# Pair matrices of the switched attention multiplied with two tiles at a time

## Chip, cores and metric

The kernel runs on one core of a Trainium2 chip. The metric is the device time of one execution in microseconds (us); lower is better.

## What is computed

The reference is a stack of eight blocks on x of shape (128, 64, 128), each added to x through a gate. Only the last one matters here, a switched attention with 8 heads, 8 experts a head and two of them chosen a row, once for the values and once for the output:

```python
gate_v = _get_sel_gate(x, sel_v_w, rs)          # sigmoid, top 2 of 8, normed
gate_o = _get_sel_gate(x, sel_o_w, rs)
q = jnp.einsum('bsd,hpd->bhsp', x, q_w.reshape(H, P, D))
k = jnp.einsum('bsd,hpd->bhsp', x, k_w.reshape(H, P, D))
xv = jnp.einsum('bsd,hedp->bshep', x, v_w.reshape(H, E, D, P))
v = jnp.einsum('bshep,bshe->bhsp', xv, gate_v)
att = jax.nn.softmax(jnp.einsum('bhqp,bhkp->bhqk', q, k) * SCALE, axis=-1)
ctx = jnp.einsum('bhqk,bhkp->bqhp', att, v)
weighted = ctx[:, :, :, None, :] * gate_o[..., None]
out = jnp.einsum('bshep,hepd->bsd', weighted, o_w.reshape(H, E, P, D))
```

Here x is layer-normed before it goes in.

## The kernel before

The earlier blocks fill the first 1210 us or so of the execution and are not touched. The last block is `switch_attention`. It works on 64 tiles of 128 rows (two sequences of 64). It is written as a software pipeline by hand: each engine has a list of steps with a lag, and `straight` walks slots t = 0, 1, 2, ... and in each slot runs every step of the list, in the order of the list, for tile t - lag. All waits are semaphores between engines; each engine runs its list in order.

What happens to a tile, with the lag before the change:

- lag 0 and 1: DVE and POOL work out the layer norm; `turn_x` (TensorE, into `sw_m`) turns the tile, and `keep_x` (ACT) copies it out of `sw_m` twice, as `sw_xT` and, rounded, as `sw_xT_high`. `low_x` (POOL) makes `sw_xT_low`, the difference of the two.
- lag 1: `logits` and `exp_logits` give the routing logits, and 20 small DVE operations, `route` (R[0] to R[19], lines 2126 to 2147), the gates. `pair_keys` (TensorE) multiplies the turned tile with the eight pair matrices `sw_pair` (query matrix times key matrix of a head, kept in f32), four heads into each of the two banks `sw_w`; `keep_u` (ACT) copies each bank to `sw_uT`; `scores` multiplies that with the turned tile.
- lag 2: the v units. A unit (`unit`, line 2221) is one head: six matmuls of 128x512, three into a bank `sw_a` and three into a bank `sw_d` (high times high, high times low, low times high), with two banks of each kind in turn. ACT scales the four experts of `sw_a` (`scale`, line 1962), DVE the four of `sw_d` and adds them up (`mix`, line 2117), and POOL adds the rest (`add_v`, lines 1889 and 1894) to give `sw_v`. `context` (line 2267) multiplies the values with the turned probabilities, into the same two banks `sw_w`, and needs `sw_v` of all eight heads.
- lag 3: the o units, the same with the context, and `add_o` on POOL. `finish` on POOL at lag 4.

A unit may start only when the unit two before it has been scaled and mixed (its banks), and ACT may scale a unit only when POOL has added the unit four before it (the four buffers `sw_scaled`). TensorE's list in a slot is

```python
stages = vs[:2] + [(1, turn_x), turns[0], vs[2], turns[1], (1, logits), vs[3], vs[4], (1, pair_keys(0))]
stages += [vs[5], (1, pair_keys(1)), vs[6], vs[7], os[0], (1, scores), os[1], (2, context)]
stages += os[2:]
```

and POOL's is add_v(0), add_v(1), low_x, finish, add_v(2) to add_v(7), add_o(1) and on.

## Time and profile before

| | |
|---|---|
| Time, median of 3 runs | 3166.97 us (3166.52 to 3173.21) |
| The profiled execution | 3168.74 us, of it a span of 3167.0 us |
| Busy: PE, PEld | 2907.0 us (92%), 2176.0 us (69%) |
| Busy: DVE, ACT, POOL | 2780.7 us (88%), 2341.8 us (74%), 2322.8 us (73%) |
| Mean granted TensorE clock | 0.941 |

PE is TensorE's matmuls, PEld its weight loads, DVE is VectorE, ACT ScalarE and POOL GpSimd. Busy is the time in which at least one instruction of the engine ran. A matmul's end is modelled and neighbours overlap, so waits shorter than some tenths of a microsecond don't show as idle on PE; they are read from the distance between starts.

### The profile page before, as it was taken

Reading aid. Unit: us, or ns where it says so; the run is one execution under the profiler, and the core shown is the slowest. Engines: PE = TensorE matmul, PEld = TensorE weight load, DVE = VectorE, ACT = ScalarE, POOL = GpSimd, SP = SyncE. Lnnn points to the kernel's source line nnn. Section 1 sums busy time; section 2 is a strip of 40 time slices with the busy share of each in tenths; the row PEclk is TensorE's granted clock in tenths of the full one; section 3 lists DMA queues with packets and bytes.
Section 4 is the critical chain, followed back from the end, with each engine's and each line's share of the span. In section 5 each row is a group of like instructions: output and inputs, shape, how many; then the busy total and the mean of one; then the engine's idle time right before and its main releaser. Section 6 shows DMA issues by size and latency. Waiting matters only on the chain.

```text
span 3167.0 us, 78218 instructions
## 1 busy us (share of the span) xinstructions
PE 2907.0 (92%) x24620; PEld 2176.0 (69%) x24620; DVE 2780.7 (88%) x9085; ACT 2341.8 (74%) x7546; POOL 2322.8 (73%) x3112
## 2 busy tenths in 40 slices
PE   7489992897689996999999999999999999999998
PEld 7257762675357774677777777777777777777776
DVE  6789997899989986888888888898898898898897
ACT  4866668888976665777777777777777777777776
POOL 2799994666876662677777777777777777777777
PEclk8589995898789997999999999999999999999999
DMA  4000000220000004100000000000000000000000
GB/s 131 8 2 2 2 2 18 68 75 13 1 6 16 16 16 109 30 9 8 7 9 8 7 9 8 7 9 8 7 9 8 8 9 8 7 9 8 7 8 6
DMA packets 114508, 55.31 MB, mean 17 GB/s; under 512 B 18352, under 2 KB 113712, under 8 KB 114096
## 3 DMA queue, kind: packets, MB, share of 16 engines
q1 hardware_dynamic: 114096, 50.30, 5.8%
q8 instruction: 200, 3.28, 0.4%
q14 instruction: 212, 1.74, 0.2%
HBM read 41.81 MB, written 8.45 MB: 16 GB/s over the span
## 4 chain that ended last, share of the span: by engine, by line
PE 59%; DVE 1%; ACT 1%; POOL 1%; DMA 0%; issue 0%; SPq 0%; POOLq 0%; ACTq 0%; DVEq 0%
PE ps_sw_a L2221 24%; PE ps_sw_d L2221 22%; PE ps_sw_w L2267 4%; PE ps_sw_w L2254 3%; PE ps_sw_s L2236 2%; PE ps_sw_s L2278 2%; PE ps_sw_m L2243 1%; ACT sw_scaled L1962 0%; DVE sw_v_part L2117 0%; PE ps_sw_m L2229 0%; DMA sw_v<-in_L_ffn_v_w 0%; POOL sw_v_pair L1889 0%; DVE sw_v_low L2056 0%; DVE sw_o_low L2063 0%; ACT sw_v_high L2017 0%
## 5 line engine op out<-in xcount | busy, mean ns | idle before, releaser
L1962 ACT ACTIVATE sw_scaled<-ps_sw_a,sw_gate_o 128x128 f32<-128x128 f32 x2048 | 620.3, 447 | 254.1 <-PE ps_sw_a L2221 247.0
L1962 ACT ACTIVATE sw_scaled<-ps_sw_a,sw_gate_v 128x128 f32<-128x128 f32 x2048 | 597.3, 448 | 196.2 <-PE ps_sw_a L2221 194.4
L2117 DVE SCALAR_TENSOR_TENSOR sw_o_part<-ps_sw_d,sw_gate_o,sw_o_part 128x128 f32<-128x128 f32 x1920 | 555.6, 339 | 63.1 <-PE ps_sw_d L2221 60.5
L1889 POOL TENSOR_TENSOR sw_v_pair<-sw_v_part,sw_scaled 128x256 f32<-128x256 f32 x512 | 381.9, 746 | 157.0 <-DVE sw_v_part L2117 91.6
L2117 DVE SCALAR_TENSOR_TENSOR sw_v_part<-ps_sw_d,sw_gate_v,sw_scaled 128x128 f32<-128x128 f32 x1024 | 303.9, 337 | 126.1 <-PE ps_sw_d L2221 107.1
L1915 POOL TENSOR_TENSOR sw_o_rest<-sw_o_rest,sw_scaled 128x256 f32<-128x256 f32 x384 | 285.4, 743 | 158.0 <-ACT sw_scaled L1962 120.7
L2117 DVE SCALAR_TENSOR_TENSOR sw_v_part<-ps_sw_d,sw_gate_v,sw_v_part 128x128 f32<-128x128 f32 x1024 | 304.8, 339 | 0.0
L1918 POOL TENSOR_TENSOR sw_o_rest<-sw_o_rest,sw_scaled 128x256 f32<-128x256 f32 x384 | 282.6, 736 | 30.1
L1894 POOL TENSOR_TENSOR sw_v<-sw_v_pair 128x128 f32<-128x128 f32 x512 | 244.6, 478 | 40.1
L1014 POOL TENSOR_TENSOR at_key_wide<-at_keyT,c_half_heads 128x1024 f32<-128x1024 f32 x128 | 242.6, 1895 | 4.6 <-ACT at_keyT L1112 4.6
L2221 PE MATMUL ps_sw_a<-sw_v_high,sw_xT_high 128*128 128x512 f32 x512 | 234.5, 458 | 8.2 <-DVE sw_v_low L2056 8.2
L2221 PE MATMUL ps_sw_a<-sw_o_high,sw_ctx_high 128*128 128x512 f32 x512 | 215.7, 421 | 0.2 <-ACT sw_scaled L1962 0.2
L2221 PE MATMUL ps_sw_d<-sw_v_high,sw_xT_high 128*128 128x512 f32 x512 | 207.6, 405 | 0.3 <-DVE sw_v_part L2117 0.3
L2221 PE MATMUL ps_sw_d<-sw_o_high,sw_ctx_high 128*128 128x512 f32 x512 | 202.1, 395 | 1.2 <-DVE sw_v_part L2117 1.2
L2221 PE MATMUL ps_sw_d<-sw_o_low,sw_ctx_high 128*128 128x512 f32 x512 | 202.7, 396 | 0.0
L2221 PE MATMUL ps_sw_a<-sw_o_high,sw_ctx_low 128*128 128x512 f32 x512 | 202.7, 396 | 0.0
L2221 PE MATMUL ps_sw_a<-sw_v_high,sw_xT_low 128*128 128x512 f32 x512 | 202.5, 396 | 0.0
L2221 PE MATMUL ps_sw_a<-sw_v_low,sw_xT_high 128*128 128x512 f32 x512 | 202.2, 395 | 0.0
L2221 PE MATMUL ps_sw_d<-sw_o_high,sw_ctx_low 128*128 128x512 f32 x512 | 202.1, 395 | 0.0
L2221 PE MATMUL ps_sw_a<-sw_o_low,sw_ctx_high 128*128 128x512 f32 x512 | 202.1, 395 | 0.0
L2221 PE MATMUL ps_sw_d<-sw_v_high,sw_xT_low 128*128 128x512 f32 x512 | 201.8, 394 | 0.0
L2221 PE MATMUL ps_sw_d<-sw_v_low,sw_xT_high 128*128 128x512 f32 x512 | 200.7, 392 | 0.0
...
## 6 DMA issues: line engine op xcount, KB each, us to landing
re_values<-in_ctx SPq DMA_DIRECT2D x128, 64.0 KB, 2.4
...
```

What stands on the lines that cost most here:

```text
L1014: pool.tensor_tensor(key_wide[:, s], keyT[:, s].unsqueeze(1).broadcast_to([P, HALF, P]), C["half_heads"][:].unsqueeze(2).broadcast_to([P, ...
L1889: pool.tensor_tensor(v_pair[:, h % 2], v_part[:, h], scaled[:, h % 4, 2:4], ALU.add)\
L1894: pool.tensor_tensor(v[:, h], v_pair[:, h % 2, 0], v_pair[:, h % 2, 1], ALU.add).then_inc(q["v"], 1)
L1915: pool.tensor_tensor(o_rest[:, 0:2], o_rest[:, 0:2], scaled[:, h % 4, 0:2], ALU.add)\
L1918: pool.tensor_tensor(o_rest[:, 2:4], o_rest[:, 2:4], scaled[:, h % 4, 2:4], ALU.add)\
L1962: act.activation(scaled[:, h % 4, e], ps_a[h % 2][:, e], ACT.Copy, scale=gates[:, s, h, HALF_E + e:HALF_E + e + 1]).then_inc(a_scaled[kind ...
L2117: dve.scalar_tensor_tensor(out=acc[:, e % 2], in0=ps_d[h % 2][:, e], scalar=gates[:, s, h, e:e + 1], in1=before, op0=ALU.mult, op1=ALU.add ...
L2221: m = pe.matmul(bank, lhs[a], w[b][:, h, experts], start=c == 0, stop=c == 2)
L2236: m = pe.matmul(ps_s[t, h], probs[t, s, h], C["ident"][t, t], start=True, stop=True)
L2254: m = pe.matmul(ps_w[n][:, h * P:(h + 1) * P], W["pair"][:, 4 * n + h], xT[:, s], start=True, stop=True)
L2267: m = pe.matmul(ps_w[b][:, h * S:(h + 1) * S], v[t, h], probs_T[t, h], start=True, stop=True)
L2278: m = pe.matmul(ps_s[t], xT[:, s, t], uT[:, :, t], start=True, stop=True)
```

## The change

`pair_keys` takes two turned tiles at once: each pair matrix is loaded once for 256 columns, where it was loaded once a tile for 128. It runs only for even tiles, in two groups of four matmuls of 128x256: heads 0 to 3 at the end of the even slot in which the second tile was turned (lag 2), heads 4 to 7 in the middle of the odd slot after (lag 3). `keep_u` becomes four copies for each pair of tiles, two at the start of the odd slot and two in its middle. Since two tiles must be turned before, everything behind `turn_x` comes two slots later: v units at lag 4, o units at lag 5, `finish` at lag 6. `sw_xT` has four buffers. The rounded copy is taken out of `keep_x` and becomes `round_x`, at lag 3, from `sw_xT` and behind v unit 4 in ACT's list. The routing buffers are shared and `sw_place` is read with a broadcast, to make room in SBUF.

```diff
-        xT = k.sb("sw_xT", [P, 2, P])
+        xT = k.sb("sw_xT", [P, 4, P])
...
-        uT = k.sb("sw_uT", [P, SH, P])
+        uT = k.sb("sw_uT", [P, SH, 2, P])
...
+        def of_pair(step):
+            def at(i, s, rd):
+                if i % 2 == 0:
+                    step(i, s, rd)
+            return at
...
-                straight([(0, fetch), (1, only_first(fetch_v)), (1, only_first(fetch_o(0, 4))), (2, fetch_residual),
-                          (2, only_first(fetch_o(4, 10))), (3, only_first(fetch_o(10, 16))), (4, store)])
+                straight([(0, fetch), (1, only_first(fetch_v)), (1, only_first(fetch_o(0, 4))), (4, fetch_residual),
+                          (2, only_first(fetch_o(4, 10))), (3, only_first(fetch_o(10, 16))), (6, store)])
...
-                stages = [(2, add_v(0)), (2, add_v(1)), (1, low_x), (4, finish)] + [(2, add_v(h)) for h in range(2, SH)]
-                stages += [(3, add_o(h)) for h in range(6)] + [(0, rstd)] + [(3, add_o(h)) for h in range(6, SH)]
+                stages = [(4, add_v(0)), (4, add_v(1)), (3, low_x), (6, finish)] + [(4, add_v(h)) for h in range(2, SH)]
+                stages += [(5, add_o(h)) for h in range(6)] + [(0, rstd)] + [(5, add_o(h)) for h in range(6, SH)]
...
                 def keep_x(i, s, rd):
                     act.wait_ge(q["x_turned"], i + 1)
+                    if not first(i, 4):
+                        act.wait_ge(q["scores"], i - 3)
+                        act.wait_ge(q["xT_low"], i - 3)
+                    act.activation(xT[:, i % 4], ps_m[:, 0], ACT.Copy).then_inc(q["xT"], 1)
+
+                def round_x(i, s, rd):
+                    act.wait_ge(q["xT"], i + 1)
                     if not first(i, 2):
-                        act.wait_ge(q["scores"], i - 1)
                         act.wait_ge(q["xT_low"], i - 1)
                         act.wait_ge(d_made["v"], SH * (i - 1))
-                    act.activation(xT[:, s], ps_m[:, 0], ACT.Copy).then_inc(q["xT"], 1)
-                    act.activation(xT_high[:, s], ps_m[:, 0], ACT.Copy).then_inc(q["xT_high"], 1)
+                    act.activation(xT_high[:, s], xT[:, i % 4], ACT.Copy).then_inc(q["xT_high"], 1)
...
                 def keep_u(n):
                     def step(i, s, rd):
                         act.wait_ge(q["u"], 2 * i + n + 1)
-                        if n == 0 and not first(i, 1):
+                        if n == 0 and i:
                             act.wait_ge(q["scores"], i)
-                        act.activation(uT[:, 4 * n:4 * n + 4], ps_w[n].rearrange("p (h t) -> p h t", h=4), ACT.Copy)\
-                            .then_inc(q["uT"], 1)
-                    return step
+                        act.activation(uT[:, 2 * n:2 * n + 2], ps_w[n % 2].rearrange("p (h c t) -> p h c t", h=2, c=2),
+                                       ACT.Copy).then_inc(q["uT"], 1)
+                    return of_pair(step)
...
-                exps = [(1, lambda i, s, rd, lo=lo: exp_scores(i, s, rd, lo)) for lo in range(0, SH, 2)]
-                vs, os = ([(lag, scale(kind, h)) for h in range(SH)] for kind, lag in (("v", 2), ("o", 3)))
-                stages = vs[:2] + [(1, keep_x)] + vs[2:4] + [(1, exp_logits), (2, keep_probs)] + vs[4:6]
-                stages += [(1, keep_u(0)), vs[6], (1, keep_u(1)), vs[7]] + os[:3] + [(2, keep_ctx(0)), os[3], exps[0]]
-                stages += [os[4], (2, keep_ctx(1)), os[5], exps[1], os[6], exps[2], os[7], exps[3]]
+                exps = [(3, lambda i, s, rd, lo=lo: exp_scores(i, s, rd, lo)) for lo in range(0, SH, 2)]
+                vs, os = ([(lag, scale(kind, h)) for h in range(SH)] for kind, lag in (("v", 4), ("o", 5)))
+                stages = [(3, keep_u(0)), vs[0], (3, keep_u(1)), vs[1], (1, keep_x)] + vs[2:4] + [(3, exp_logits), (4, keep_probs)]
+                stages += [vs[4], (3, round_x), vs[5], (3, keep_u(2)), vs[6], (3, keep_u(3)), vs[7]] + os[:3]
+                stages += [(4, keep_ctx(0)), os[3], exps[0], os[4], (4, keep_ctx(1)), os[5], exps[1], os[6], exps[2], os[7], exps[3]]
...
-                            lambda: dve.tensor_tensor(r["eq1"][:], r["p"][:], wide(rm["m1"][:]), ALU.is_equal),
-                            lambda: dve.tensor_tensor(r["w1"][:], r["eq1"][:], place[:], ALU.mult),
...
+                            lambda: dve.tensor_tensor(r["equal"][:], p[:], wide(rm["m1"][:]), ALU.is_equal),
+                            lambda: dve.tensor_tensor(r["equal"][:], r["equal"][:], place[:].unsqueeze(1).broadcast_to(G), ALU.mult),
...
-                R = [[(1, route(n))] for n in range(RANK)]
+                         for kind, lag in (("v", 4), ("o", 5)) for h in range(SH)}
+
+                R = [[(3, route(n))] for n in range(RANK)]
...
                 def turn_x(i, s, rd):
                     pe.wait_ge(q["xhat"], i + 1)
-                    if not first(i, 1):
-                        pe.wait_ge(q["decays"], i)
+                    if i >= 1:
+                        pe.wait_ge(q["xT"], i)
+                    if i >= 3:
+                        pe.wait_ge(q["decays"], i - 2)
                     pe.transpose(ps_m[:, 0], L["xhat"][:, s], C["ident"][:]).then_inc(q["x_turned"], 1)
...
-                    pe.wait_ge(q["xT_high"], i + 1)
-                    pe.matmul(ps_m[:, 1], xT[:, s], W["sel"][:], start=True, stop=True).then_inc(q["logits"], 1)
-
-                def pair_keys(n):
+                    pe.wait_ge(q["xT"], min(i + 3, TILES))
+                    pe.matmul(ps_m[:, 1], xT[:, i % 4], W["sel"][:], start=True, stop=True).then_inc(q["logits"], 1)
+
+                def pair_keys(lo):
                     def step(i, s, rd):
-                        if i == 0:
-                            pe.wait_ge(prep["kept"], 2 + n)
-                        elif not first(i, 2):
-                            pe.wait_ge(q["ctx_low"], 2 * (i - 2) + n + 1)
-                        else:
-                            pe.wait_ge(q["uT"], 1 + n)
-                        for h in range(4):
-                            m = pe.matmul(ps_w[n][:, h * P:(h + 1) * P], W["pair"][:, 4 * n + h], xT[:, s],
-                                          start=True, stop=True)
-                        m.then_inc(q["u"], 1)
-                    return step
+                        if lo == 0:
+                            pe.wait_ge(q["xT"], i + 2)
+                        for n in (lo, lo + 1):
+                            if n >= 2:
+                                pe.wait_ge(q["uT"], 2 * i + n - 1)
+                            elif i == 0:
+                                pe.wait_ge(prep["kept"], 3)
+                            else:
+                                pe.wait_ge(q["ctx_low"], 2 * (i - 2) + n + 1)
+                            both = xT[:, i % 4:i % 4 + 2].rearrange("p c t -> p (c t)")
+                            for h in range(2):
+                                m = pe.matmul(ps_w[n % 2][:, 2 * h * P:2 * (h + 1) * P], W["pair"][:, 2 * n + h], both,
+                                              start=True, stop=True)
+                            m.then_inc(q["u"], 1)
+                    return of_pair(step)
...
                 def context(i, s, rd):
-                    upto = min(i + 2, TILES) if isinstance(i, int) else i + 2
-                    wait_alone(pe, (q["v"], SH * i + SH), (q["p_kept"], i + 1), (q["uT"], 2 * upto))
-                    if isinstance(i, int) and i == TILES - 1:
+                    wait_alone(pe, (q["v"], SH * i + SH), (q["p_kept"], i + 1))
+                    if i % 2 and i < TILES - 1:
+                        pe.wait_ge(q["uT"], 2 * (i + 3))
+                    elif i:
                         pe.wait_ge(q["ctx_low"], 2 * i)
+                    else:
+                        pe.wait_ge(q["uT"], 4)
...
-                    waits = [(q["uT"], 2 * i + 2)]
+                    waits = [(q["uT"], 4 * (i // 2) + 4)]
...
-                        m = pe.matmul(ps_s[t], xT[:, s, t], uT[:, :, t], start=True, stop=True)
+                        m = pe.matmul(ps_s[t], xT[:, i % 4, t], uT[:, :, s, t], start=True, stop=True)
...
-                vs, os = ([(lag, unit(kind, h)) for h in range(SH)] for kind, lag in (("v", 2), ("o", 3)))
-                turns = [(2, lambda i, s, rd, lo=lo: turn_probs(i, s, rd, lo)) for lo in (0, 4)]
-                stages = vs[:2] + [(1, turn_x), turns[0], vs[2], turns[1], (1, logits), vs[3], vs[4], (1, pair_keys(0))]
-                stages += [vs[5], (1, pair_keys(1)), vs[6], vs[7], os[0], (1, scores), os[1], (2, context)]
-                stages += os[2:]
+                vs, os = ([(lag, unit(kind, h)) for h in range(SH)] for kind, lag in (("v", 4), ("o", 5)))
+                turns = [(4, lambda i, s, rd, lo=lo: turn_probs(i, s, rd, lo)) for lo in (0, 4)]
+                stages = vs[:2] + [(1, turn_x), turns[0], vs[2], turns[1], (3, logits), vs[3], vs[4], (3, pair_keys(2))]
+                stages += vs[5:] + [os[0], (3, scores), os[1], (4, context)] + os[2:] + [(2, pair_keys(0))]
```

TensorE in a middle slot, before, from v unit 4 to v unit 6 (sw_w is the bank of `pair_keys`); the same rows stand in every slot:

```order
L2221 MATMUL ps_sw_d<-sw_v_high,sw_xT_low 128x512
L2254 MATMUL ps_sw_w<-sw_xT,sw_pair 128x128 x4
L2221 MATMUL ps_sw_a<-sw_v_high,sw_xT_high 128x512
L2221 MATMUL ps_sw_a<-sw_v_low,sw_xT_high 128x512
L2221 MATMUL ps_sw_a<-sw_v_high,sw_xT_low 128x512
L2221 MATMUL ps_sw_d<-sw_v_high,sw_xT_high 128x512
L2221 MATMUL ps_sw_d<-sw_v_low,sw_xT_high 128x512
L2221 MATMUL ps_sw_d<-sw_v_high,sw_xT_low 128x512
L2254 MATMUL ps_sw_w<-sw_xT,sw_pair 128x128 x4
```

TensorE of the changed kernel, an odd slot, from the end of v unit 4; an even slot has no row of `sw_pair` here, and has this row behind its last o unit instead:

```order
L2233 MATMUL ps_sw_d<-sw_v_low,sw_xT_high 128x512
L2233 MATMUL ps_sw_d<-sw_v_high,sw_xT_low 128x512
L2272 MATMUL ps_sw_w<-sw_xT,sw_pair 128x256 x4
L2233 MATMUL ps_sw_a<-sw_v_high,sw_xT_high 128x512
L2233 MATMUL ps_sw_a<-sw_v_low,sw_xT_high 128x512
```

So the even slot's middle loses both groups, the odd slot's middle keeps one of twice the columns, and the end of the even slot gains one.

ACT in the first half of a slot, before:

```order
L1962 ACTIVATE sw_scaled<-ps_sw_a,sw_gate_v 128x128 x8
L1972 ACTIVATE sw_xT<-ps_sw_m 128x128
L1973 ACTIVATE sw_xT_high<-ps_sw_m 128x128
L1962 ACTIVATE sw_scaled<-ps_sw_a,sw_gate_v 128x128 x8
L1985 ACTIVATE sw_exp<-ps_sw_m 128x128
L1979 ACTIVATE sw_probs_T<-ps_sw_s 128x512
L1962 ACTIVATE sw_scaled<-ps_sw_a,sw_gate_v 128x128 x8
```

and in the same place of an even slot of the changed kernel:

```order
L1968 ACTIVATE sw_scaled<-ps_sw_a,sw_gate_v 128x128 x8
L1977 ACTIVATE sw_xT<-ps_sw_m 128x128
L1968 ACTIVATE sw_scaled<-ps_sw_a,sw_gate_v 128x128 x8
L1996 ACTIVATE sw_exp<-ps_sw_m 128x128
L1990 ACTIVATE sw_probs_T<-ps_sw_s 128x512
L1968 ACTIVATE sw_scaled<-ps_sw_a,sw_gate_v 128x128 x4
L1984 ACTIVATE sw_xT_high<-sw_xT 128x128
L1968 ACTIVATE sw_scaled<-ps_sw_a,sw_gate_v 128x128 x12
```

`sw_xT_high` has moved from behind two v units (eight activations) to behind five. POOL's list has not moved: `low_x`, which reads `sw_xT_high`, still stands behind add_v(1), with `finish` and add_v(2) to add_v(7) behind it.

## Rows read from the trace of the kernel before

**Rows 1.** Windows: length, busy us of PE, PEld, DVE, ACT, POOL; clock, DMA share, GB/s.
```profile
1313.44:3091.00 1777.56, 1777.23 (x10982) 1361.00 (x10980) 1595.50 (x5701) 1353.20 (x5283) 1359.30 (x2101) 1.00 0.03 8
```

**Rows 2.** Tile sw_xhat: turn_x, one a slot, durations ns, first and last start.
```profile
L2229 PE MATMUL ps_sw_m<-c_ident,sw_xhat x64: 270/271/477, 1225.1 to 3091.0; 128*128 128x128 f32 x64
```

**Rows 3.** Timeline, PE, one slot: start us, us, engine line op out<-in.
```profile
2030.58 1.05 PE L2254 MATMUL ps_sw_w<-sw_xT,sw_pair 128*128 128x128 f32 x8
2031.39 0.48 PE L2221 MATMUL ps_sw_a<-sw_v_high,sw_xT_high 128*128 128x512 f32 x1
2031.70 0.40 PE L2221 MATMUL ps_sw_a<-sw_v_low,sw_xT_high 128*128 128x512 f32 x1
2031.93 0.39 PE L2221 MATMUL ps_sw_a<-sw_v_high,sw_xT_low 128*128 128x512 f32 x1
...
2040.25 0.39 PE L2221 MATMUL ps_sw_d<-sw_o_high,sw_ctx_low 128*128 128x512 f32 x1
2040.73 2.00 PE L2267 MATMUL ps_sw_w<-sw_probs_T,sw_v 64*128 64x64 f32 x32
```

**Rows 4.** Line 1894: who waited for sw_v (us, times).
```profile
  PEld ps_sw_w L2267: 32.1, 64
```

**Rows 5.** Timeline, DVE, same slot, v units 3 to 7.
```profile
2029.82 0.61 DVE L2117 SCALAR_TENSOR_TENSOR sw_v_part<-ps_sw_d,sw_gate_v,sw_scaled 128x128 f32<-128x128 f32 x2 [1.52 <-ACT sw_scaled L1962]
...
2033.29 0.59 DVE L2117 SCALAR_TENSOR_TENSOR sw_v_part<-ps_sw_d,sw_gate_v,sw_scaled 128x128 f32<-128x128 f32 x2
...
2034.93 0.81 DVE L2132 TENSOR_TENSOR sw_r_sel<-sw_r_w,sw_m_w 128x128 f32<-128x128 f32 x1
...
2036.18 0.28 DVE L2133 SCALAR_TENSOR_TENSOR sw_r_p<-sw_r_sel,sw_r_p 128x128 f32<-128x128 f32 x1
...
2038.65 0.60 DVE L2117 SCALAR_TENSOR_TENSOR sw_v_part<-ps_sw_d,sw_gate_v,sw_v_part 128x128 f32<-128x128 f32 x2
```

**Rows 6.** Timeline, POOL, same slot.
```profile
2028.06 0.46 POOL L1881 TENSOR_TENSOR sw_xT_low<-sw_xT,sw_xT_high 128x128 fp32r<-128x128 f32 x1
...
2030.53 0.72 POOL L1889 TENSOR_TENSOR sw_v_pair<-sw_v_part,sw_scaled 128x256 f32<-128x256 f32 x1
...
2031.75 0.74 POOL L1889 TENSOR_TENSOR sw_v_pair<-sw_v_part,sw_scaled 128x256 f32<-128x256 f32 x1
...
2039.40 0.74 POOL L1889 TENSOR_TENSOR sw_v_pair<-sw_v_part,sw_scaled 128x256 f32<-128x256 f32 x1 [1.00 <-DVE sw_v_part L2117]
2040.22 0.46 POOL L1894 TENSOR_TENSOR sw_v<-sw_v_pair 128x128 f32<-128x128 f32 x1
```

**Rows 7.** Timeline, ACT, same slot.
```profile
2030.37 1.18 ACT L1962 ACTIVATE sw_scaled<-ps_sw_a,sw_gate_v 128x128 f32<-128x128 f32 x4
2032.37 1.14 ACT L1962 ACTIVATE sw_scaled<-ps_sw_a,sw_gate_v 128x128 f32<-128x128 f32 x4 [0.82 <-PE ps_sw_a L2221]
2033.38 0.62 ACT L1993 ACTIVATE sw_uT<-ps_sw_w 128x512 f32<-128x512 f32 x1
```

**Rows 8.** Timeline, PE, start of the slot: the two halves of v unit 0.
```profile
2021.49 0.47 PE L2221 MATMUL ps_sw_a<-sw_v_high,sw_xT_high 128*128 128x512 f32 x1
...
2022.26 0.49 PE L2221 MATMUL ps_sw_d<-sw_v_high,sw_xT_high 128*128 128x512 f32 x1
```

**Rows 9.** Timeline, ACT and PE, the beginning of the block.
```profile
1225.77 0.27 ACT L1973 ACTIVATE sw_xT_high<-ps_sw_m 128x128 fp32r<-128x128 f32 x1
...
1236.00 2.04 ACT L2017 ACTIVATE sw_v_high<-sw_v_part 128x1024 fp32r<-128x1024 f32 x2
...
1250.09 0.48 PE L2229 MATMUL ps_sw_m<-c_ident,sw_xhat 128*128 128x128 f32 x1 [6.76 <-DVE sw_xhat L259]
...
1313.44 0.27 PE L2229 MATMUL ps_sw_m<-c_ident,sw_xhat 128*128 128x128 f32 x1
```

**Rows 10.** Timeline, DVE, two of the 16 pieces of o weights.
```profile
1251.71 0.68 DVE L2063 TENSOR_TENSOR sw_o_low<-sw_o_part,sw_o_high 128x512 fp32r<-128x512 f32 x1
1253.49 0.69 DVE L2063 TENSOR_TENSOR sw_o_low<-sw_o_pair,sw_o_high 128x512 fp32r<-128x512 f32 x1
```

42 lines of the change are left out of this document (21 added, 21 removed).

## The prediction

> **What bounds the kernel now.** The rows by engine over the middle of the last block come first: from 1313.44 to 3091.0 us TensorE is busy 1777.23 of 1777.56 us at a granted clock of 1.00, VectorE 90% and POOL and ACT 76% each [rows 1]. So TensorE looks like the only bound. `turn_x` runs once a slot; from 1313.44 to 3091.0 there are 60 slots, 29.63 us each [rows 2, 9]. But the profile's matmuls overlap, and shares don't say what TensorE's order is tied to. For that I read one slot on every engine, the one from 2021.5 to 2051, and all times of day below are of it.
>
> The reader is to see a second chain that takes as long as TensorE's. `context` needs `sw_v` of all heads. POOL's last add of the v units ends at 2040.22 + 0.46 = 2040.68, and `context` starts at 2040.73 [rows 3, 6]; after a first-bank matmul the usual distance is some 0.33 us, so 2040.58 would have been TensorE's own time. Over the whole run its weight load waited for that add 64 times, 0.5 us each [rows 4]: the two meet in every slot with about a tenth of a us between them. Behind POOL stands VectorE: its v units 3 to 7 with the routing between them run without an idle row from 2029.82 to 2038.65 + 0.60 = 2039.25 [rows 5], and POOL's last add waited 1.00 us for it [rows 6]. From 2029.82 to `context` neither has room.
>
> **What the change does to each part.**
>
> *The pair matrices themselves.* A group of four 128x128 matmuls takes 2031.39 - 2030.58 = 0.81 us, and the next matmul's successor comes after 0.31 instead of 0.23 us [rows 3], so 0.89 us a group and 3.56 us for the four groups of two tiles. A group of four of 256 columns does the same columns as two of these: at most 1.78 us, and if the extra 0.08 us of the restart is paid once, 1.70. I take 1.74, so 3.48 us for two tiles: 0.08 us saved in a pair of slots. Halving the weight loads saves nothing further, since PEld is 77% busy beside a full PE [rows 1].
>
> *Even slot, middle.* Here 1.78 us of matmuls go away between v unit 4 and v unit 6. TensorE would be ready for `context` at 2038.8. VectorE's chain is not shortened: it had no idle, so v unit 7 is mixed at 2039.25 and `sw_v` complete at 2040.68 as before. The two groups were covered by VectorE's work, and taking them away gives nothing here.
>
> *Even slot, end.* The new group stands behind the last o unit, where TensorE has nobody's work to hide behind: 1.74 us on the path. It covers something: the halves of v unit 0 start 2022.26 - 2021.49 = 0.77 us apart [rows 8], where three matmuls of 0.23 take 0.69 [rows 3]. That 0.08 us is a wait for the last o units to be scaled and mixed; all four halves of v units 0 and 1 have one, some 0.3 us together, which the group absorbs. Net 1.45 us a pair of slots.
>
> *The rounded copy.* This is the step that I expect to cost most by itself. `low_x` on POOL started at 2028.06 [rows 6]. It will wait for `round_x`, which ACT reaches behind v unit 4: that starts at 2030.37, its successor's copy follows a unit's start by 2033.38 - 2032.37 = 1.01 us [rows 7], so `round_x` runs from 2031.38 and, at the 0.27 us of the same copy with nothing beside it [rows 9], ends at 2031.65. Queued behind `low_x` on POOL are `finish` and add_v(2) to add_v(7). From the start of `low_x` to that of add_v(2) are 2.47 us, from one add_v to the next 1.22, and the last takes 1.28 to the end of `sw_v` [rows 6]. So: 2031.70 + 2.47 + 5 x 1.22 + 1.28 = 2041.55, `context` at 2041.60. TensorE's own time is 2040.58: 1.0 us late, in every slot. POOL's slack of 2.6 us (its waits for ACT and VectorE between the adds) is what the other part of the delay of 3.6 us goes into. For the port (next paragraph) I add 0.1: 1.1 us in even slots.
>
> *Port.* VectorE's L2132 took 0.81 us, against 0.28 for L2133 of the same shape and also with two inputs in SBUF [rows 5]; it lay beside a POOL add, of 0.74 us [rows 6]. Two of the routing operations in this stretch are so long in each slot. With POOL busy without a pause from 2031.7 to 2041.6 some more of the routing will meet an add; I take 0.4 us more on VectorE, which the even slot hides.
> The Trainium skill (SBUF — State Buffer, Terms) says that VectorE and GpSimd share a port pair that is locked for the whole instruction, "the loser fully blocks"; by that rule, read strictly, each of VectorE's two-input operations in this stretch could lose up to an add's 0.74 us. The trace agrees for L2132 and not for most others, so it is a rival below and not the sum.
>
> *Odd slot, middle.* One group of 1.74 us stands before v unit 5, where 0.89 stood before and 0.89 after it. V unit 5 comes 0.85 us later on TensorE, so its mix, before at 2033.29 [rows 5], starts at about 2034.1 and VectorE, without slack, ends v unit 7 at 2040.05; with 0.4 us for the port, 2040.45. POOL gets to that add at 2031.70 + 2.47 + 5 x 1.22 = 2040.27, so it waits 0.2 more, and any more on VectorE goes through: 1.1 + 0.3 = 1.4 us in odd slots.
>
> *No cost.* The four `keep_u` of an odd slot are as many copies as the two of each slot before; the two at its start fall into the time that ACT gains by the group. `sw_place` by broadcast and routing in place keep the number and shape of operations. `logits` waits for the next but one tile's `keep_x`, which stands where it stood.
>
> *Beginning and end.* Two more slots without matmul units. Rounding of the v weights began at 1236.00, behind the exponentials of tile 0, though tile 0 was turned and copied at 1226 [rows 9]; these now come two slots later, so the weights are ready up to 9 us sooner. Against this, the 16 pieces of o weights, before beside units, now stand before the first unit: VectorE's first two are 1.78 us apart [rows 10], of which the units between took half; at 1.4 us each 22 us, and 4 us of routing and exponentials. `turn_x` of the first slot with units: 1250 - 9 + 22 + 4 = 1267. That slot has no o units: 22 us, and the next 30.9. The steady state begins at 1320 instead of 1313.4: 7 us, between -5 and +20. The end is the same chain of units as before.
>
> **The sum.** A pair of slots costs 1.1 + 1.4 + 1.45 = 3.95 us; 0.08 us saved is already in the 1.74. There are 31 such pairs: 122 us. With 7 for the beginning, 129 us on a span of 3167.0 gives 3296. The profiled execution took 3168.74 us and the median is 3166.97, so I give the median as 3296 us. Its own range is 3262 to 3325: the end term lies between 1.2 and 1.78, the two context terms between 0.9 and 1.8.
>
> **The rivals.**
>
> *Only one of the two terms appears.* If ACT or POOL have room that I don't see (a faster restart of the adds, `round_x` earlier because ACT is ahead in even slots), only the group at the slot's end counts: 31 x 1.45 + 7 = 52, 3219 us. If VectorE and POOL are so late at the end of the slot that they take the group in, only POOL's chain counts: 31 x 2.5 + 7 = 85, 3252 us. For it: the chain's slack was read from one slot. Against it: rows 4 says that all slots are alike. 0.20.
>
> *VectorE becomes the bound through the port.* If all six of its two-input operations between 2033 and 2039 lose the 0.53 us that L2132 loses against L2133, and not two as now, VectorE is 4 x 0.53 = 2.1 us later. V unit 7 is then mixed at 2041.35 in even slots and 2042.15 in odd ones, `context` follows 1.28 + 0.15 us later, 2.2 and 3.0 us behind 2040.58; with the end term 6.65 us a pair, 31 x 6.65 + 7 = 213, 3380 us. Two more instead of four: 1.2 + 2.0 + 1.45 = 4.65, 3318 us, inside the forecast's own range. The port rule of the page above would make this case. 0.12.
>
> *It ends faster.* One mechanism: the slot border. If `round_x` is not late for POOL, that is, if it ends before 2028.1 + 2.6 = 2030.7, the chain to `context` stays where it was, and if in even slots VectorE's v units can start as much earlier as the group at the end gave it time, the 1.78 us are found again; then a pair saves the 0.3 us of the border and 0.08: 31 x 0.38 = 12, 3155 us with no loss at the beginning. It decides for faster when VectorE's 9.4 us chain from 2029.82 can start 1.5 us sooner; its wait of 1.52 us there was for ACT's scaling of v unit 3, which TensorE's own order sets, and that speaks against it. 0.08, and 0.05 for landing within 0.2% by the same road with the 7 us lost.
>
> **How the numbers follow.** Forecast 0.55, one term only 0.20, port 0.12, slot border 0.13. 3205 to 3335 us leaves out the border case and most of the port case. A measurement of this kernel can tell some 0.2% (6 us) from no change. Faster 0.08, same 0.05, slower 0.87.
>
> **What would show it.** In the profile after: `turn_x` to `turn_x` of some 32.2 us from an even slot to the odd one and some 31.0 the other way; idle rows of POOL before `low_x` of some 3 us for ACT `sw_xT_high`; `context` starting just behind the last add of `sw_v`, and more than 0.33 us behind the o matmul before it; v unit 7 of even slots ready on TensorE well before VectorE mixes it. Wrong if the two slots of a pair take 59.3 us together, if POOL's wait is short, or if VectorE has idle rows between v units 4 and 7 of an even slot.

## The result and the profile after

The changed kernel takes 3328.23 us, the median of 4 runs (3321.27 to 3330.93), against 3167.64 us for the kernel before, run on the same chip (4 runs, 3166.52 to 3173.21). The ratio is 1.05, with a 95% interval of 1.048 to 1.052: it is slower by 161 us. The forecast was 3296 us in a range of 3205 to 3335; the narrower range that the sum gave for itself, 3262 to 3325, is missed by 3 us.

The profiled execution took 3321.27 us, with a span of 3319.5. Busy times and the chain that ended last, from its page:

```profile
span 3319.5 us, 77191 instructions
PE 2953.5 (89%) x24108; PEld 2159.5 (65%) x24108; DVE 2806.3 (85%) x9085; ACT 2346.8 (71%) x7546; POOL 2313.8 (70%) x3112
PE 33%; POOL 12%; issue 7%; DVE 5%; ACT 4%; DMA 1%; POOLq 0%; SPq 0%; DVEq 0%; ACTq 0%
```

The middle of the last block by engine, as in [rows 1]; and `turn_x`, as in [rows 2]:

```profile
1322.80:3175.59 1852.79, 1760.35 (x10152) 1300.76 (x10150) 1567.21 (x5512) 1310.86 (x5107) 1311.65 (x2031) 0.99 0.03 7
```
```profile
L2243 PE MATMUL ps_sw_m<-c_ident,sw_xhat x64: 270/270/476, 1222.9 to 3175.6; 128*128 128x128 f32 x64
```

TensorE is now idle for 92 of 1853 us, where it was idle for less than one. The 58 slots of this stretch take 31.94 us each against 29.63. They alternate: all 29 odd slots take 31.09 us; of the even ones 22 take 32.40 us and seven 33.9 to 34.3.

Who TensorE's matmuls wait for, from the table of waits (us in total, times, longest):

```profile
PE ps_sw_w L2288 <- POOL sw_v L1900: 41.3, 63, 4.1
PE ps_sw_d L2233 <- DVE sw_v_part L2128: 29.7, 61, 0.8
PE ps_sw_a L2233 <- ACT sw_scaled L1968: 29.4, 33, 1.2
```

None of the three was among the ten largest before. One even slot follows, from its `turn_x` at 1769.18 to the next at 1801.54. POOL, to be read against [rows 6]:

```profile
1772.23 0.55 POOL L1900 TENSOR_TENSOR sw_v<-sw_v_pair 128x128 f32<-128x128 f32 x1
1776.51 0.46 POOL L1887 TENSOR_TENSOR sw_xT_low<-sw_xT,sw_xT_high 128x128 fp32r<-128x128 f32 x1 [3.73 <-ACT sw_xT_high L1984]
...
1778.99 0.72 POOL L1895 TENSOR_TENSOR sw_v_pair<-sw_v_part,sw_scaled 128x256 f32<-128x256 f32 x1
...
1786.14 0.45 POOL L1900 TENSOR_TENSOR sw_v<-sw_v_pair 128x128 f32<-128x128 f32 x1
```

After add_v(1) POOL stands 3.73 us for the rounded copy, and from then on works without a pause until `sw_v` is complete at 1786.59. `low_x` starts 7.33 us behind `turn_x`, where it started 3.56 behind it; add_v(2) starts 2.48 us behind `low_x`, as before. Next ACT, VectorE and TensorE of the same slot:

```profile
1776.06 0.38 ACT L1984 ACTIVATE sw_xT_high<-sw_xT 128x128 fp32r<-128x128 f32 x1
...
1779.81 2.36 ACT L1968 ACTIVATE sw_scaled<-ps_sw_a,sw_gate_v 128x128 f32<-128x128 f32 x8 [2.34 <-POOL sw_v_pair L1895]
```
```profile
1780.53 0.61 DVE L2128 SCALAR_TENSOR_TENSOR sw_v_part<-ps_sw_d,sw_gate_v,sw_scaled 128x128 f32<-128x128 f32 x2 [0.67 <-ACT sw_scaled L1968]
```
```profile
1781.09 0.47 PE L2233 MATMUL ps_sw_a<-sw_o_high,sw_ctx_high 128*128 128x512 f32 x1 [0.93 <-ACT sw_scaled L1968]
...
1786.65 2.00 PE L2288 MATMUL ps_sw_w<-sw_probs_T,sw_v 64*128 64x64 f32 x32 [0.90 <-POOL sw_v L1900]
```

POOL's delay reaches TensorE twice. ACT may not scale v unit 6 before POOL has freed the buffers of unit 2: it waits 2.34 us, VectorE 0.67 behind it, and o unit 0 starts 0.93 us late. Then `context` waits 0.90 us for the last add. It starts 17.47 us behind `turn_x`, against 16.10 before. Only the second wait sets this time: POOL has no pause between `low_x` and the end of `sw_v`, and VectorE is done with v unit 7 early. In 26 even slots POOL's last add starts 1.19 us behind VectorE's last row of that unit on average, where it was 0.14 before. In the odd slot behind it:

```profile
1808.87 0.45 POOL L1887 TENSOR_TENSOR sw_xT_low<-sw_xT,sw_xT_high 128x128 fp32r<-128x128 f32 x1 [4.32 <-ACT sw_xT_high L1984]
...
1817.79 0.74 POOL L1895 TENSOR_TENSOR sw_v_pair<-sw_v_part,sw_scaled 128x256 f32<-128x256 f32 x1 [0.28 <-DVE sw_v_part L2128]
```
```profile
1807.62 1.89 PE L2272 MATMUL ps_sw_w<-sw_xT,sw_pair 128*128 128x256 f32 x8
1809.16 0.58 PE L2233 MATMUL ps_sw_a<-sw_v_high,sw_xT_high 128*128 128x512 f32 x1
1809.58 0.40 PE L2233 MATMUL ps_sw_a<-sw_v_low,sw_xT_high 128*128 128x512 f32 x1
...
1819.11 2.00 PE L2288 MATMUL ps_sw_w<-sw_probs_T,sw_v 64*128 64x64 f32 x32 [0.29 <-POOL sw_v L1900]
```

`context` starts 17.57 us behind `turn_x`. The last add has waited 0.28 us for VectorE. VectorE starts v unit 5 at 9.43 us behind `turn_x`, against 8.65 before (means), and loses as much again by the end of v unit 7, where its routing operations meet POOL's adds. One of them, with the add that it meets:

```profile
1813.89 0.80 DVE L2145 SCALAR_TENSOR_TENSOR sw_r_p<-sw_r_sel,sw_exp 128x128 f32<-128x128 f32 x1
```
```profile
1813.79 0.75 POOL L1895 TENSOR_TENSOR sw_v_pair<-sw_v_part,sw_scaled 128x256 f32<-128x256 f32 x1
```

The six two-input routing operations between the rows of v units 4 and 7 last 3.64 us together in odd slots and 2.64 in even ones, against 2.94 before (means).

On TensorE a group of 256 columns takes 1.54 us to the next matmul, whose successor comes after 0.42 instead of 0.23: 1.73 us, as estimated.

Where the 152.5 us of the span went:

| | us |
|---|---|
| Two slots of a pair together 63.48 against 59.26; 29 pairs | 122.4 |
| Seven even slots with a fall of the granted clock, 1.5 to 1.9 more each | 11.8 |
| `turn_x` of the first slot with all units at 1322.8, before at 1313.4 | 9.4 |
| Last `turn_x` to the end: 143.9 against 76.0 and two slots of 29.63 (some two pairs' worth) | 8.7 |

The block itself began 2.2 us sooner than before (first `turn_x` at 1222.9, before at 1225.1), so its beginning costs 11.6 us, of which the earlier blocks gave 2.2 back. Over all runs the first `turn_x` lies between 1220.8 and 1228.6.

### The profile page after: what moved, and what is told of

The parts are those of the page before. It is cut to its first block, busy times and chain, and to the rows that moved or that the text cites. A ratio compares the mean times of both kernels' runs of the same rounds, so it can differ in the third digit from the quotient of the medians.

```text
span 3319.5 us, 77191 instructions
## 1 busy us (share of the span) xinstructions
PE 2953.5 (89%) x24108; PEld 2159.5 (65%) x24108; DVE 2806.3 (85%) x9085; ACT 2346.8 (71%) x7546; POOL 2313.8 (70%) x3112
## 3 DMA queue, kind: packets, MB, share of 16 engines
q14 instruction: 211, 1.73, 0.2%
## 4 chain that ended last, share of the span: by engine, by line
PE 33%; POOL 12%; issue 7%; DVE 5%; ACT 4%; DMA 1%; POOLq 0%; SPq 0%; DVEq 0%; ACTq 0%
PE ps_sw_a L2233 12%; PE ps_sw_d L2233 10%; PE ps_sw_w L2288 4%; ACT sw_scaled L1968 4%; POOL sw_o_rest L1921 3%; POOL sw_o_rest L1924 3%; DVE sw_v_part L2128 3%; PE ps_sw_w L2272 3%; POOL sw_v_pair L1895 2%; PE ps_sw_s L2299 2%; PE ps_sw_s L2250 1%; DVE sw_r_p L2145 1%; POOL sw_v L1900 1%; POOL sw_o_pair L1933 1%; POOL sw_o_pair L1931 1%
## 5 line engine op out<-in xcount | busy, mean ns | idle before, releaser
L2233 PE MATMUL ps_sw_d<-sw_o_high,sw_ctx_high 128*128 128x512 f32 x512 | 212.4, 415 | 29.5 <-DVE sw_v_part L2128 29.2
L1887 POOL TENSOR_TENSOR sw_xT_low<-sw_xT,sw_xT_high 128x128 fp32r<-128x128 f32 x64 | 29.9, 467 | 260.1 <-ACT sw_xT_high L1984 260.1
```

The source lines that it names most:

```text
L2233: m = pe.matmul(bank, lhs[a], w[b][:, h, experts], start=c == 0, stop=c == 2)
```

## The experiments

Two theories stood: **A**, the late rounding holds POOL's queue, and the group at the end of even slots stands bare, each on its own; **B**, one of the two, or the port alone, accounts for the loss. All kernels were timed against the kernel before, whose median was 3168.7, 3171.78 or 3170.29 us on the three chips used. "Even" and "odd" are slots; the last two columns say how long after `turn_x` the start of `context` comes. All four are means of some 26 slots, without the slots in which the clock fell. The kernel before moves by up to 4 us from chip to chip, and differences of kernels from different chips are no better than that.

| kernel | us (lowest, highest) | ratio, 95% interval | even, odd slot | context, even, odd |
|---|---|---|---|---|
| before | 3167.64 | | 29.63, 29.63 | 16.10, 16.10 |
| after | 3328.23 | 1.05 (1.048, 1.052) | 32.40, 31.09 | 17.49, 17.56 |
| e1_round_early | 3245.51 (3237.03, 3246.07) | 1.023 (1.021, 1.0251) | 30.93, 30.43 | 16.02, 16.88 |
| e3_low_last | 3234.01 (3231.9, 3238.89) | 1.0202 (1.0183, 1.0221) | 30.81, 30.32 | 15.91, 16.78 |
| e4_before_round_late | 3275.69 (3271.21, 3280.84) | 1.0332 (1.0312, 1.0352) | 31.06 all | 17.51, 17.51 |
| e2_round_mid | 3274.87 (3271.61, 3276.96) | 1.0327 (1.0311, 1.0342) | 31.85, 30.47 | 16.95, 16.95 |
| e5_end_group_small | 3201.05 (3196.99, 3205.26) | 1.0092 (1.0071, 1.0113) | 29.68, 30.32 | 16.02, 16.77 |
| e6_spare_group_even | 3265.39 (3260.45, 3267.49) | 1.0295 (1.028, 1.0311) | 31.71, 30.39 | 16.80, 16.87 |
| e7_routing_small | 3180.68 (3173.91, 3182.52) | 1.0026 (1.0016, 1.0036) | 29.86, 29.57 | 14.95, 16.01 |
| e8_routing_later | 3189.83 (3185.13, 3191.22) | 1.0057 (1.0042, 1.0072) | 30.08, 29.65 | 15.02, 16.01 |
| e9_mid_group_later | 3224.07 (3220.72, 3224.7) | 1.0168 (1.0154, 1.0182) | 31.19, 29.58 | 16.27, 16.00 |
| e10_all_mended | 3197.54 (3193.27, 3198.82) | 1.0081 (1.0067, 1.0094) | 30.35, 29.66 | 15.30, 16.01 |
| e11_before_routing_later | 3170.34 (3167.14, 3174.16) | 0.9999 (0.999, 1.0008) | 29.72 all | 16.09, 16.09 |

### Where the rounded copy stands

**e1_round_early**: the changed kernel, with `round_x` right behind `keep_x`.

```diff
-                stages = [(3, keep_u(0)), vs[0], (3, keep_u(1)), vs[1], (1, keep_x)] + vs[2:4] + [(3, exp_logits), (4, keep_probs)]
-                stages += [vs[4], (3, round_x), vs[5], (3, keep_u(2)), vs[6], (3, keep_u(3)), vs[7]] + os[:3]
+                stages = [(3, keep_u(0)), vs[0], (3, keep_u(1)), vs[1], (1, keep_x), (3, round_x)] + vs[2:4] + [(3, exp_logits), (4, keep_probs)]
+                stages += [vs[4], vs[5], (3, keep_u(2)), vs[6], (3, keep_u(3)), vs[7]] + os[:3]
```

> The changed kernel with round_x moved up in ACT's list, from behind v unit 4 to right behind keep_x; nothing else. Theory (POOL's adds were held by low_x): low_x starts some 3.6 us sooner, POOL no longer sets context. In even slots context comes back to 16.1 us behind turn_x; in odd slots VectorE is still 0.85 us late because the pair group stands before v unit 5, so 16.9 to 17.0. The group at the slot's end still costs 1.4. A pair of slots: 59.26 + 0.85 + 1.4 = 61.5 instead of 63.5, no short falls of the clock: about 3247 us. Rival 1 (slots are set by TensorE's own instructions alone, the rounding has nothing to do with it): unchanged, 3328 us. Rival 2 (port: VectorE is held by POOL's adds): less than half of the gain, above 3290 us.

83 us come back by moving one activation. `context` of even slots starts 16.02 us behind `turn_x`, about as before, though the middle of the slot has 1.78 us less on TensorE; that of odd slots comes 0.86 us later than in even ones (0.78 later than before the change), and the even slot is still long at its end.

**e3_low_last** leaves ACT's list alone and moves the step that waits: POOL's `low_x` goes behind add_v(7).

```diff
-                stages = [(4, add_v(0)), (4, add_v(1)), (3, low_x), (6, finish)] + [(4, add_v(h)) for h in range(2, SH)]
+                stages = [(4, add_v(0)), (4, add_v(1)), (6, finish)] + [(4, add_v(h)) for h in range(2, SH)] + [(3, low_x)]
```

> The changed kernel with low_x moved back in POOL's list, from behind add_v(1) to behind add_v(7); ACT's list as changed, so the rounding stays late. Theory (what costs is the queue behind low_x on POOL and not the rounding itself): the same as with the early rounding, about 3247 us, with sw_xT_high still at 6.9 us behind turn_x. Rival 1 (ACT's order costs, its late copy pushes v unit 5 back): 3300 us or more. Rival 2 (low_x at the end is too late for the next slot's v unit 0, which needs sw_xT_low): TensorE waits at the slot's start, above 3328 us.

The copy is as late as in the changed kernel (6.89 us behind `turn_x`), and the loss is gone all the same. So it is POOL's queue behind `low_x` that costs, not the lateness of the copy or ACT's time for it.

**e4_before_round_late** puts the late copy alone into the kernel before: none of the pair groups moves.

```diff
-                    act.activation(xT_high[:, s], ps_m[:, 0], ACT.Copy).then_inc(q["xT_high"], 1)
+
+                def round_x(i, s, rd):
+                    act.wait_ge(q["xT"], i + 1)
+                    act.activation(xT_high[:, s], xT[:, s], ACT.Copy).then_inc(q["xT_high"], 1)
...
-                stages = vs[:2] + [(1, keep_x)] + vs[2:4] + [(1, exp_logits), (2, keep_probs)] + vs[4:6]
+                stages = vs[:2] + [(1, keep_x)] + vs[2:4] + [(1, exp_logits), (2, keep_probs)] + [vs[4], (1, round_x), vs[5]]
...
-                    pe.wait_ge(q["xT_high"], i + 1)
+                    pe.wait_ge(q["xT"], i + 1)
```

> The kernel before with this part of the change alone: the rounded copy taken out of keep_x, made from sw_xT and placed behind v unit 4 in ACT's list. Pair matrices, lags and buffers as before. Theory: context comes 1.1 to 1.4 us later in every one of some 63 slots, 69 to 88 us, and up to 15 us more from short falls of TensorE's clock behind its waits: 3236 to 3270 us. Rival 1 (POOL has room, or the cost needs the new order of the pair groups): 3167 us. Rival 2 (port): more than 3300 us.

It costs 107 us by itself, a little more than expected. Its group of `low_x`, and the wait of TensorE:

```profile
L1881 POOL TENSOR_TENSOR sw_xT_low<-sw_xT,sw_xT_high 128x128 fp32r<-128x128 f32 x64 | 29.5, 461 | 243.2 <-ACT sw_xT_high L1976 243.2
```
```profile
PE ps_sw_w L2270 <- POOL sw_v L1894: 62.8, 64, 6.0
```

Every slot takes 31.06 us, 1.43 more, but for 11 slots of 32.5 to 33.0. In the one of these whose windows were read, the granted clock is 0.56 to 0.58 for 4 us. At 1.43 us each, 63 slots are 90 us, where 69 to 88 were expected; the 11 cost another 18 us, where up to 15 were expected. The part does alone what it does in the whole: `context` comes at 17.51 us here, and at 17.49 in even slots of the changed kernel.

**e2_round_mid** puts `round_x` between the two places, ahead of `exp_logits`.

```diff
-                stages = [(3, keep_u(0)), vs[0], (3, keep_u(1)), vs[1], (1, keep_x)] + vs[2:4] + [(3, exp_logits), (4, keep_probs)]
-                stages += [vs[4], (3, round_x), vs[5], (3, keep_u(2)), vs[6], (3, keep_u(3)), vs[7]] + os[:3]
+                stages = [(3, keep_u(0)), vs[0], (3, keep_u(1)), vs[1], (1, keep_x)] + vs[2:4] + [(3, round_x), (3, exp_logits), (4, keep_probs)]
+                stages += [vs[4], vs[5], (3, keep_u(2)), vs[6], (3, keep_u(3)), vs[7]] + os[:3]
```

> The changed kernel with round_x behind v unit 3, ahead of exp_logits, one v unit earlier than in the change. It should start at about 5.2 us behind turn_x and low_x at 5.7, so POOL's last add ends at 5.7 + 2.47 + 5 x 1.23 + 1.28 = 15.6, just ahead of VectorE's path (16.0). Theory (POOL has a slack, and only what goes beyond it costs): no later than with the early rounding, about 3245 us, though low_x is still 2.1 us later than in the kernel before. Rival (every delay of low_x goes through): half-way between, some 3285 us.

A miss by 30 us. `low_x` came where expected and POOL is not the bound: its last add waits 1.00 us for VectorE. VectorE itself is 0.93 us later than in e1 in even slots. Two routing operations of one even slot, first e1 and then this kernel:

```profile
1757.38 0.31 DVE L2142 TENSOR_TENSOR sw_r_equal<-sw_r_equal,sw_place 128x128 f32<-128x128 f32 x1
...
1759.68 0.27 DVE L2145 SCALAR_TENSOR_TENSOR sw_r_p<-sw_r_sel,sw_exp 128x128 f32<-128x128 f32 x1
```
```profile
1769.18 0.79 DVE L2142 TENSOR_TENSOR sw_r_equal<-sw_r_equal,sw_place 128x128 f32<-128x128 f32 x1
...
1771.64 0.80 DVE L2145 SCALAR_TENSOR_TENSOR sw_r_p<-sw_r_sel,sw_exp 128x128 f32<-128x128 f32 x1
```

In the second kernel each starts inside one of POOL's long adds. In the first, L2145 meets none and L2142 only the last 0.15 us of one. In even slots the six two-input operations last 3.50 us together, against 2.96 in e1. The rest of the 0.93 us is there already when VectorE starts v unit 4, 0.38 us later than in e1; how much of that is the later exponential was not tested. Moving POOL's work by 2 us changed which VectorE operations meet it.

### The pair groups

**e5_end_group_small** is e1 with the group at the end of even slots cut to two matmuls of 16 columns. The output leaves out the scores of heads 0 to 3.

```diff
+                                if lo == 0 and i:
+                                    if h:
+                                        m = pe.matmul(ps_w[n % 2][:, 0:16], W["pair"][:, 2 * n], xT[:, i % 4, 0:16],
+                                                      start=True, stop=True)
+                                    continue
```

> The early-rounding version with the group at the end of even slots cut to two matmuls of 16 columns (heads 0 to 3 of the scores are therefore not computed but for the first pair of tiles); all semaphores and copies stay. Theory (the group lies uncovered at the slot's end and costs 1.4 us net): 30 x 1.4 = 42 us faster than the early-rounding version, about 3205 us. Rival 1 (the last o units are so late on ACT and VectorE that they cover it): no difference. Rival 2 (it costs more than its own length through the banks sw_w): more than 55 us faster.

The even slot is 1.25 us shorter, 39 us over 31 pairs; the median fell by 44, and where the other 5 come from is not shown. Of the group's 1.73 us at least 1.25 show: it is nearly bare.

**e6_spare_group_even** is e1 with an unused group of the same size behind v unit 4 of even slots, where the first of the two groups stood that the change had taken away.

```diff
+                def spare_group(i, s, rd):
+                    if i % 2 or i == 0:
+                        return
+                    pe.wait_ge(q["ctx_low"], 2 * i)
+                    both = xT[:, i % 4:i % 4 + 2].rearrange("p c t -> p (c t)")
+                    for n in range(2):
+                        for h in range(2):
+                            pe.matmul(ps_w[n][:, 2 * h * P:2 * (h + 1) * P], W["pair"][:, 2 * n + h], both, start=True, stop=True)
...
-                stages = vs[:2] + [(1, turn_x), turns[0], vs[2], turns[1], (3, logits), vs[3], vs[4], (3, pair_keys(2))]
+                stages = vs[:2] + [(1, turn_x), turns[0], vs[2], turns[1], (3, logits), vs[3], vs[4], (3, pair_keys(2)), (4, spare_group)]
```

> The early-rounding version with a further group of four 128x256 matmuls with pair matrices put behind v unit 4 of every even slot, its result unused: 1.74 us of TensorE work 31 times. Theory (TensorE's time in the even middle is covered by VectorE's units and routing): context of even slots stays at 16.0 and the time at 3245 us, at most 10 us more (VectorE's v unit 5 may come late, as in odd slots: then 16.9 and 3270). Rival (TensorE is the bound in the even middle): 31 x 1.74 = 54 us more, 3299 us.

20 us, not 54: of 1.73 us more on TensorE only 0.78 reach `context`. They do so through VectorE, which now gets v unit 5 late:

```profile
1770.35 0.61 DVE L2128 SCALAR_TENSOR_TENSOR sw_v_part<-ps_sw_d,sw_gate_v,sw_scaled 128x128 f32<-128x128 f32 x2 [0.70 <-PE ps_sw_d L2233]
```

The even slot now has in its middle what the odd one has, and its `context` comes as late (16.80 and 16.87 us).

### Is it VectorE that holds the middle?

**e7_routing_small** is e1 with the routing comparisons R[3] to R[11] on 2 of the 16 groups of experts; it leaves out the choice of experts for the others.

```diff
-                            lambda: dve.tensor_tensor(r["equal"][:], p[:], wide(rm["m1"][:]), ALU.is_equal),
+                            lambda: dve.tensor_tensor(r["equal"][:, 0:2], p[:, 0:2], wide2(rm["m1"][:, 0:2]), ALU.is_equal),
...
-                            lambda: dve.tensor_reduce(rm["m2"][:], r["p2"][:], AX.X, ALU.max),
+                            lambda: dve.tensor_reduce(rm["m2"][:, 0:2], r["p2"][:, 0:2], AX.X, ALU.max),
...
```

> The early-rounding version with eleven of the 20 routing operations (R[3] to R[11], R[12] stays whole) on 2 of the 16 groups of 8 only: gates are therefore mostly wrong, all other work is kept. It takes about 1.5 to 2 us of VectorE work out of the stretch between v units 4 and 7. Theory (there VectorE sets context): in even slots context comes at 14.3 to 15.0 instead of 16.0, in odd ones at 16.0 to 16.3 instead of 16.9: 30 x (1.0 to 1.7 + 0.6 to 0.9), 3165 to 3195 us. Rival (TensorE or POOL set it): no change, 3245 us.

**e8_routing_later** does all of the work, but later: e1, with R[6] and on spread over fewer v units, and R[8] to R[11] among the o units.

```diff
-                    "v": [[], [], [(4, sums(0))], [(4, sums(1))], [(4, sums(2))], [], *R[0:5], R[5] + R[6], R[7],
-                          R[8] + R[9], R[10], R[11]],
-                    "o": [R[12], R[13] + R[14], R[15] + R[16], [(3, peak)], [(3, shifts)], R[17], R[18],
+                    "v": [[], [], [(4, sums(0))], [(4, sums(1))], [(4, sums(2))], [], *R[0:5], R[5], [],
+                          R[6], [], R[7]],
+                    "o": [R[8], R[9] + R[10], R[11] + R[12], [(3, peak)], [(3, shifts)], R[13], R[14],
```

> The early-rounding version with nothing left out, but VectorE's routing operations R[8] to R[11] moved out of the stretch of the v units into that of the o units, the rest behind them. Theory: context earlier as in the small-routing run, part of it given back because VectorE is then later at the end of odd slots: 3175 to 3215 us. It can't come below the kernel before by much, as the group at the slot's end and the beginning stay. Rival: VectorE gets so late in the stretch of the o units that TensorE waits there, 3245 us or more.

Both came out inside what was expected: with VectorE's chain shorter, `context` of even slots moves 1.0 us forward and of odd slots 0.87. So some 1.1 of the 1.78 us of matmuls taken out of the even middle show at last. In e8 `sw_v` is complete 0.92 us ahead of `context` in even slots, and what TensorE waits for there is a bank `sw_d` that VectorE has not yet mixed, at v unit 6 (29 times in the 29 even slots, 8.1 us in all):

```profile
1746.70 0.50 PE L2233 MATMUL ps_sw_d<-sw_v_high,sw_xT_high 128*128 128x512 f32 x1 [0.25 <-DVE sw_v_part L2128]
```

**e9_mid_group_later** is e3 with the middle group of odd slots one unit later, so that VectorE gets v unit 5 in time.

```diff
-                stages = vs[:2] + [(1, turn_x), turns[0], vs[2], turns[1], (3, logits), vs[3], vs[4], (3, pair_keys(2))]
-                stages += vs[5:] + [os[0], (3, scores), os[1], (4, context)] + os[2:] + [(2, pair_keys(0))]
+                stages = vs[:2] + [(1, turn_x), turns[0], vs[2], turns[1], (3, logits), vs[3], vs[4], vs[5], (3, pair_keys(2))]
+                stages += vs[6:] + [os[0], (3, scores), os[1], (4, context)] + os[2:] + [(2, pair_keys(0))]
```

> The version with low_x behind add_v(7), and the middle group of odd slots moved from ahead of v unit 5 to behind it. Theory (odd slots lose 0.85 us because VectorE, without slack, gets v unit 5 late): v unit 5 is early now and v unit 6 starts where it started before the change, so context of odd slots comes at 16.0 instead of 16.8: 30 x 0.8 = 24 us less than 3234, about 3210 us. Rival (the delay of odd slots is POOL's or the port's): no change, 3234 us.

Of the 24 us expected only half came: 3224 us, where 3210 were expected. The odd slot gave all of its part (`context` at 16.00 instead of 16.78), but the even slot, which the edit does not touch, lost 0.38 us. One VectorE operation goes with it. Two even slots of this same kernel, one of 30.78 us and the next one of 31.35 us, on VectorE and POOL:

```profile
1815.45 0.23 DVE L2138 TENSOR_SCALAR sw_exp<-sw_exp 128x128 f32<-128x128 f32 x1
...
1875.82 0.75 DVE L2138 TENSOR_SCALAR sw_exp<-sw_exp 128x128 f32<-128x128 f32 x1
```
```profile
1815.50 0.78 POOL L1895 TENSOR_TENSOR sw_v_pair<-sw_v_part,sw_scaled 128x256 f32<-128x256 f32 x1
...
1875.74 0.74 POOL L1895 TENSOR_TENSOR sw_v_pair<-sw_v_part,sw_scaled 128x256 f32<-128x256 f32 x1
```

In the first VectorE starts 0.05 us ahead of POOL's add and takes 0.23 us; in the second it starts 0.08 us behind it and takes 0.75, to just behind the add's end at 1876.48. Of 26 even slots, the 20 in which it lasted 0.75 or 0.80 us took 31.12 to 31.35 us, the six with 0.23 took 30.77 to 30.84. In e3 it is 0.23 in 24 of 26.

**e10_all_mended** is e9 with the later routing of e8.

> The last version (low_x last, middle group behind v unit 5) with the later routing as well; every part of the change that was found to cost is mended but the group at the end of even slots. Theory: odd slots 29.6 us, even slots 29.6 - 1.1 + 1.4 = 29.9 to 30.0, 59.6 us a pair against 59.26, plus some 8 us at the beginning: 3175 to 3190 us, still not faster than the kernel before. Rival (even slots reach TensorE's own 14.4 us to context): 59.0 us a pair, 3165 us.

A miss: 8 us above the upper end of what was expected, and no better than e8, which has fewer repairs. Odd slots are as in e8; in even slots the same operation takes 0.69 to 0.76 us where e8 has 0.41 to 0.46 (25 of 26 slots in each), and `context` is 0.28 us later. Over 30 even slots that is the 8 us.

**e11_before_routing_later** asks whether easing POOL's and VectorE's chain helps the kernel before: `low_x` last and the later routing, no pair group moved.

> The kernel before with the two mends that don't need the change: low_x behind add_v(7), and the routing operations R[8] to R[11] and those behind them moved into the stretch of the o units. Theory (before the change TensorE and the chain of VectorE and POOL are level, so easing the second gives at most the 0.1 us by which context waits in some slots and part of the 0.3 us at the border): 3150 to 3170 us. Rival (VectorE gets late in the stretch of the o units): 3180 us or more.

No difference. `sw_v` is now complete 1.16 us ahead of `context`, as one slot shows (`turn_x` at 1816.87; POOL, then TensorE):

```profile
1831.33 0.46 POOL L1894 TENSOR_TENSOR sw_v<-sw_v_pair 128x128 f32<-128x128 f32 x1
```
```profile
1832.95 2.00 PE L2267 MATMUL ps_sw_w<-sw_probs_T,sw_v 64*128 64x64 f32 x32
```

and `context` starts 16.08 us behind `turn_x`, where it was at 16.10. So TensorE's own time was 16.1 all along, and the second chain ended just ahead of it. None of the versions beats the kernel before.

## Why the prediction was nearly right, step by step

The mechanism, its places and most sizes held. A pair of slots was to cost 3.95 us and costs 4.22; 31 pairs (29 in the middle and the 8.7 us of the end) make 131 us where 122 were forecast. With 2.4 us more at the beginning and 11.8 us for the clock, which the sum does not have, that is the way from the forecast span of 3296 us to the 3319.5 of the profiled execution. The stated own range of 3262 to 3325 does not follow from the bounds given with it: 31 pairs of 3.0 and of 5.38 us, with 7 us, give 3267 and 3341.

- **The rounded copy.** `low_x` was to start 3.6 us later: 3.77. The late steps behind it were to cost 1.1 us in even slots: 1.39. The path is the one forecast, POOL's queue; two terms were too small. `round_x` beside other work took 0.38 us and not 0.27. And from the start of `low_x` to the end of `sw_v` POOL takes 10.08 us in the slot shown, without a pause, where the sum had 9.85 and 0.1 for the port: two of its adds of 128x256 took 0.78 us, the others 0.72 or 0.73. One sign of being wrong did appear, "VectorE has idle rows between v units 4 and 7 of an even slot": there is one, of 0.67 us, because the four `sw_scaled` buffers carry POOL's delay to ACT and from there to VectorE and o unit 0. The prediction did not follow this way, but it does not set the time, since VectorE is still 1.05 us ahead at the last add, and behind `context` the even slot takes the same 14.91 us in e1, where ACT has no such wait. e1 and e3 take this term away, and e4 makes it alone.
- **The port.** The 0.4 us was a guess, and the prediction misread its own slot when it held that the rule of the lock did not show in most operations. Beside L2132 of [rows 5], this is another of VectorE's, and the adds that the two meet:

```profile
2033.81 0.38 DVE L2130 TENSOR_TENSOR sw_r_w<-sw_r_eq,sw_place 128x128 f32<-128x128 f32 x1
```
```profile
2033.31 0.73 POOL L1889 TENSOR_TENSOR sw_v_pair<-sw_v_part,sw_scaled 128x256 f32<-128x256 f32 x1 [0.28 <-ACT sw_scaled L1962]
...
2034.85 0.74 POOL L1889 TENSOR_TENSOR sw_v_pair<-sw_v_part,sw_scaled 128x256 f32<-128x256 f32 x1 [0.28 <-DVE sw_v_part L2117]
```

  L2130 ends at 2034.19, 0.15 us behind the end of the first add; L2132 ends at 2035.74, 0.15 us behind the end of the second. L2133 starts while POOL is idle and takes 0.28 us. So the cost is neither nothing nor an add each time, but what is left of POOL's instruction when VectorE's starts. In the changed kernel that is 0.7 us more in odd slots and 0.3 us less in even ones (3.64, 2.64 and 2.94 us above). The term is not a constant of the kernel but depends on where the two engines' lists meet.
- **Even slot, middle.** Worth nothing, as said: e1 has `context` at 16.02. e7 and e8 show that it is VectorE that holds it, and e6 that 0.95 of a group's 1.73 us fits there unseen.
- **Odd slot, middle.** 1.4 us forecast, 1.46 measured, in part by luck. V unit 5 on its own costs 0.78 us (e1), where 0.85 were taken, and what VectorE loses behind it in the changed kernel is another 0.77, where 0.4 were taken. The slot that was read hid the difference: VectorE ends v unit 7 there at 14.75 us behind `turn_x`, and at 14.55 in the mean.
- **Even slot, end.** 1.45 us forecast. The even slot's part behind `context` is 14.91 us, against 13.53 before: 1.38. e5 gives 1.25 for the cut.
- **Beginning.** 7 us forecast, 9.4 measured, or 11.6 from the block's own start.
- **The clock.** Not in the sum: 11.8 us in the profiled execution. Of the four runs that one had the highest mean granted clock, 0.940, and the least time; the others had 0.936 to 0.938 and 3327.89 to 3330.93 us. That they have more falls is likely, but not shown.

The rival "one of the two terms only" falls with e4 and e5, which show both terms each for itself. The port rival was right in kind and wrong in reach. The rival of a faster end had 0.3 us of the border to gain, and the border gave 1.73 - 1.38 = 0.35; what it needed besides, a chain to `context` that doesn't move, is what e8 comes nearest to, and it still ends 18 us behind.

Why no repair wins can be estimated from the slots. If nothing but TensorE set the even middle, its `context` would come at 16.01 - 1.73 = 14.3, and the pair would take 14.3 + 14.91 + 29.57 = 58.8 us: 0.45 less than 59.26, or 14 us over 31 pairs, of which the beginning takes 9. No run reached this; e7 and e8 came to 15.0. Loading the weights half as often gave TensorE next to nothing by itself: a group of 256 columns takes 1.73 us, and two of 128 take 1.78.
